# Taking a norm-and-gate epilogue out of a recurrent loop and running it over all token tiles at once, behind the loop

## The reference, cut to what matters

```python
def _step(S, xs):                      # once per token, per head
    qt, kt, vt, gt, bt = xs
    S = S * jnp.exp(gt)[..., None, None]
    delta = (vt - jnp.einsum('bhk,bhkv->bhv', kt, S)) * bt[..., None]
    S = S + jnp.einsum('bhk,bhv->bhkv', kt, delta)
    return (S, jnp.einsum('bhk,bhkv->bhv', qt, S))
...
o = gated_delta_rule(q, k, v, g, beta)                    # tokens, 6 heads, 64
o = o * rsqrt(mean(o * o, over the 64) + 1e-5) * norm_weight
o = o * silu(x @ Wg)
return o.reshape(tokens, 384) @ Wo
```

## Time and profile before

| what | value |
|---|---|
| median of three runs | 1545.75 us (1544.89 to 1547.8) |
| the profiled execution's own time | 1545.75 us |
| its span in the trace | 1544.0 us, 31244 instructions |
| outside the span | 1.75 us |
| PE busy / DVE busy / ACT busy / POOL busy | 87% / 60% / 44% / 20% of the span |
| the state block | about 554 to 599.8 us |

### The profile page before, as it was taken

How to read it: one execution, slowest core, us unless ns; L and a number is a source line. 1 busy time by engine, 2 the same in 40 slices (tenths; PEclk the granted TensorE clock), 3 DMA queues, 4 the chain that set the end, 5 groups by cost and what they waited for, 6 DMA issues and landing times. The chain is left out here.

```text
span 1544.0 us, 31244 instructions
## 1 busy us (share of the span) xinstructions
PE 1339.6 (87%) x12873; PEld 752.5 (49%) x12881; DVE 919.0 (60%) x2164; ACT 681.9 (44%) x987; POOL 305.8 (20%) x394
## 2 busy tenths in 40 slices
PE   7999997987150998899999989999789999989999
PEld 3355544553130877363555545436235555555436
DVE  3899965744886246665999935433445555535431
ACT  5578786634250223644777762111334444442110
POOL 4340440001308000006100000110333434210110
PEclk9999998998665599998999998999679999998999
DMA  3222200000312100003222030000300000000000
GB/s 89 59 42 62 61 2 32 1 12 0 103 41 51 28 5 1 14 1 64 38 37 40 13 100 0 1 9 0 62 10 16 14 16 14 9 1 1 0 0 28
DMA packets 51808, 41.64 MB, mean 27 GB/s; under 512 B 26498, under 2 KB 41971, under 8 KB 51667
## 3 DMA queue, kind: packets, MB, share of 16 engines
q1 hardware_dynamic: 51666, 39.65, 11.9%
HBM read 20.33 MB, written 3.43 MB: 15 GB/s over the span
## 5 line engine op out<-in xcount | busy, mean ns | idle before, releaser
L586 DVE TENSOR_REDUCE row_max_pieces<-psum 128x1 f32<-128x512 f32 (+3 forms) x672 | 407.2, 647 | 125.0 <-PE psum L481 122.6
L685 ACT ACTIVATE probs<-psum 128x1024 f32<-128x1024 f32 (+7 forms) x384 | 343.8, 900 | 219.8 <-PE psum L481 219.4
L535 PE MATMUL psum<-probs,v_ones 128*32 128x256 f32 (+1 forms) x2688 | 239.3, 377 | 8.6 <-POOL probs L470 4.2
L481 PE MATMUL psum<-q_all,k_head 97*32 97x512 f32 (+3 forms) x1536 | 193.8, 497 | 3.5 <-issue 3.5
L481 PE MATMUL psum<-k_stack,q_stack 96*32 96x512 bf16 x2048 | 162.6, 387 | 5.5 <-DVE row_max_pieces L586 3.3
L481 PE MATMUL psum<-q_stack,k_stack 97*32 97x512 bf16 x2048 | 160.8, 385 | 0.0
L535 PEld LDWEIGHTS psum<-probs,v_ones 128*32 128x32 f32 x2688 | 88.6, 109 | 85.1 <-POOL probs L470 21.2
L481 PE MATMUL psum<-k_head_bf,q_all_bf 80*32 80x512 bf16 (+3 forms) x768 | 96.6, 349 | 5.2 <-POOL q_all_bf L2314 3.7
L481 PEld LDWEIGHTS psum<-q_all,k_head 97*32 97x32 f32 x1536 | 79.2, 110 | 34.9 <-issue 9.3
L481 PEld LDWEIGHTS psum<-k_stack,q_stack 96*32 96x32 bf16 x2048 | 58.2, 97 | 71.9 <-DVE row_max_pieces L586 20.4
L481 PEld LDWEIGHTS psum<-q_stack,k_stack 97*32 97x32 bf16 x2048 | 59.5, 97 | 50.7 <-issue 3.8
(11 more groups left out here) (324 smaller groups left out, 2096.0 us busy)
## 6 DMA issues: line engine op xcount, KB each, us to landing
q_stack<-arena SPq DMA_DIRECT2D x32, 96.0 KB, 2.7
k_stack<-arena SPq DMA_DIRECT2D x32, 96.0 KB, 2.7
arena<-gd_g_sums SPq DMA_DIRECT2D x6, 512.0 KB, 5.9
q_stack<-arena SPq DMA_DIRECT2D x32, 64.0 KB, 2.3
k_stack<-arena SPq DMA_DIRECT2D x32, 64.0 KB, 2.3
x_tokens<-in_x SPq DMA_DIRECT2D x4, 256.0 KB, 4.2
k_stack<-arena SPq DMA_DIRECT2D x32, 32.0 KB, 2.3
q_stack<-arena SPq DMA_DIRECT2D x32, 32.0 KB, 2.0
```

What stands on the lines that cost most here:

```text
L481: last = pe.matmul(o[j:j + 32], by[:, j:j + 32], rows, **flags)
L535: last = pe.matmul(psum[32 * g:32 * g + VW, PVB, a - g * D:D], V[:, c, h, :], pr[:, n % PB, a:(g + 1) * D], start=(c == 0), stop=(c == (2 ...
L586: last = dve.reduce_max(mx[:, h % 2, qt, i:i + 1], o[:, 0:plain], AX.X)
L685: act.activation(pr[:, n % PB, q_from(c):], psum[:, 2 * (n % 2):2 * (n % 2) + 2, :].rearrange("p a n -> p (a n)")[:, q_from(c):], ACT.Exp, ...
```

## The change

Four things are done.

1. POOL's eight multiplications of `SG` by the norm weight leave the gate block. The weight's load now counts on the semaphore of `Wo`'s load.
2. The state loop loses its norm: ACT's Square and Sqrt, DVE's `mean_squares` and `norm_and_gate`. ACT keeps only the copy of the outputs.
3. The wait of DVE for the constant `own_block` moves from tile 0's state spread to ahead of the loop.
4. A new block stands between the state block and `project_out`. In it POOL multiplies `SG` by the weight, eight instructions of 128x384, and DVE does the whole norm over 128x3072 in a chain in which nearly each instruction waits for the one before.

```diff
@@ gate block, gpsimd
-                            pool.wait_ge(nw_loaded, 16)
-                            for t in range(NT):
-                                pool.wait_ge(gate_out, t + 1)
-                                gated = SG[:, t].rearrange("p (h c) -> p h c", c=GV)
-                                pool.tensor_tensor(gated, gated, nw[:].unsqueeze(1).broadcast_to([P, GH, GV]), ALU.mult)
@@ state block, vector
+                        dve.wait_ge(own_in, 16)
                         dve.wait_ge(blocked, 2)
                         for t in range(NT):
...
-                            if t >= 1:
-                                mean_squares(t - 1)
...
-                            if t == 0:
-                                dve.wait_ge(own_in, 16)
...
-                            if t >= 1:
-                                norm_and_gate(t - 1)
-                        mean_squares(NT - 1)
-                        norm_and_gate(NT - 1)
@@ state block, scalar
                         for t in range(NT):
                             act.wait_ge(o_in, t + 1)
-                            if t >= 2:
-                                act.wait_ge(summed, t - 1)
-                            act.activation(sq[:, t % 2], psum[:, 2 + t % 2, 0:VWD], ACT.Square).then_inc(squared, 1)
                             act.activation(O[:, t, :], psum[:, 2 + t % 2, 0:VWD], ACT.Copy).then_inc(o_kept, 1)
-                            act.wait_ge(ms_done, t + 1)
-                            act.activation(ms[:, t], ms[:, t], ACT.Sqrt).then_inc(rooted, 1)
@@ new block
+                with nc.Block() as block:
+                    @block.gpsimd
+                    def _(pool):
+                        for t in range(NT):
+                            pool.tensor_tensor(SG[:, t].rearrange("p (h c) -> p h c", c=GV),
+                                               SG[:, t].rearrange("p (h c) -> p h c", c=GV),
+                                               nw[:].unsqueeze(1).broadcast_to([P, GH, GV]), ALU.mult).then_inc(sw, 1)
+                    @block.scalar
+                    def _(act):
+                        act.wait_ge(to_act, 1)
+                        act.activation(ms[:], ms[:], ACT.Sqrt).then_inc(from_act, 1)
+                    @block.vector
+                    def _(dve):
+                        n = [0]
+                        def link(i):
+                            n[0] += 1
+                            i.then_inc(ch, 1)
+                            dve.wait_ge(ch, n[0])
+                        link(dve.tensor_tensor(sq[:], O[:], O[:], ALU.mult))
+                        link(dve.reduce_sum(ms[:], sq[:].rearrange("p t (h c) -> p (t h) c", c=GV), AX.X))
+                        dve.tensor_scalar(ms[:], ms[:], 1.0 / GV, RMS_EPS, ALU.mult, ALU.add).then_inc(to_act, 1)
+                        dve.wait_ge(from_act, 1)
+                        link(dve.reciprocal(rr[:], ms[:]))
+                        link(dve.tensor_tensor(O[:].rearrange("p t (h c) -> p (t h) c", c=GV),
+                                               O[:].rearrange("p t (h c) -> p (t h) c", c=GV),
+                                               rr[:].unsqueeze(2).broadcast_to([P, NT * GH, GV]), ALU.mult))
+                        dve.wait_ge(sw, NT)
+                        dve.tensor_tensor(O[:], O[:], SG[:], ALU.mult)
```

More of the change, by code:

```diff
@@ L1062, in gated_delta @@
         QET = sb("qe_features", [P, 2, S])
-        wload, nw_loaded = sem("wo_loaded"), sem("norm_weight_loaded")
+        wload = sem("wo_loaded")
         with ExitStack() as mid_scope:
@@ L1142, in loads @@
                         sp.dma_start(nw[:], d["nw"].rearrange("(a n) -> a n", a=1).broadcast_to([P, GV])
-                                     ).then_inc(nw_loaded, 16)
+                                     ).then_inc(wload, 16)
                         sp.dma_start(dtb[:], d["dt"].rearrange("(a n) -> a n", a=1).broadcast_to([P, GH])
@@ L1152, in _ @@
                             loads(sp)
-                            sp.wait_ge(wload, 16)
-                            sp.wait_ge(nw_loaded, 16)
+                            sp.wait_ge(wload, 32)
                             sp.wait_ge(head_loads, 32)
@@ L1628, in gated_delta @@
                 U = sb2("u", [P, 2, VWD])
[L1629 to L1634, removed]
                 s0, u_in, u_kept, s_in, s_done, o_in, o_kept = (sem(n) for n in
@@ L1681, in _ @@
                     def _(dve):
[L1682 to L1697, removed]
                         dve.memset(St[:], 0.0).then_inc(s0, 1)
@@ L1734, in _ @@
                             act.wait_ge(o_in, t + 1)
-                            if t >= 2:
-                                act.wait_ge(summed, t - 1)
-                            act.activation(sq[:, t % 2], psum[:, 2 + t % 2, 0:VWD], ACT.Square).then_inc(squared, 1)
                             act.activation(O[:, t, :], psum[:, 2 + t % 2, 0:VWD], ACT.Copy).then_inc(o_kept, 1)
-                            act.wait_ge(ms_done, t + 1)
-                            act.activation(ms[:, t], ms[:, t], ACT.Sqrt).then_inc(rooted, 1)
+            with ExitStack() as tmp2:
+                sb2 = lambda n, shape, dt=F32: core.sb(n, shape, dt, tmp2)
+                sq = EA.rearrange("p c n -> p (c n)")[:, 0:NT * VWD].rearrange("p (t n) -> p t n", t=NT)
+                ms, rr = sb2("o_mean_squares", [P, NT * GH]), sb2("o_inverse_rms", [P, NT * GH])
+                ch, sw, to_act, from_act = sem("norm_chain"), sem("gate_weighted"), sem("rms_in"), sem("rms_out")
+                with nc.Block() as block:
[26 more added lines that the diff above has]
+                        dve.tensor_tensor(O[:], O[:], SG[:], ALU.mult)
```

## The result

The changed kernel took 1563.95 us as the median of four runs (1560.65 to 1567.48); the kernel before, beside it, 1546.32 us (1544.89 to 1547.8). The ratio is 1.0115, with a 95% interval of 1.0087 to 1.0144: slower, as forecast. Besides these four the result lists 18 more executions of the changed kernel, the profiled one (1568.8) among them; all 22 have a mean of 1564.4, from 1556.35 to 1571.83. The median lies 1.45 us above the top of the forecast range and 3.65 above the forecast itself.

The account below looks back on a forecast made before the run. PE was taken to bound the state loop, with only tile 7's norm showing. New block 17.5 - 2.15 (earlier start) - 0.80 (gate block) = +14.55 us on 1545.75 gave 1560.3 us, range 1556.8 to 1562.5.

Parts of the forecast that it names:

- The loop is PE's; the norm in it is free: State loop: PE, busy 39.47 of 40.20 us, bounds it; only tile 7's norm is on the path, 2.93 us.
- The rival that taking the norm out speeds up the loop: State loop: the norm's work was holding PE up, so removing it brings the kernel within 0.2%; chance 2%.
- Part 1: Gate block's end: without POOL's multiplications it ends with DVE, 0.80 us earlier.
- Part 2: State loop without norm: period stays 5.26 us; DVE starts the new block 2.15 us before the old end.
- Part 3: Ahead of the state loop: the wait for `own_block` costs nothing, ending 0.66 us before DVE is first needed.
- Part 4: New block: DVE's chain takes 14.5 us alone, 17.5 us with POOL's multiplications beside it.
- the mutual hold: New block: POOL and DVE's two-input multiplies hold each other up, block takes 17.5 us; chance 51%, 1560.3 us.
- rivals without a hold: New block: POOL and DVE do not hold each other up, +11.55 us, 1557.3 us; chance 13%.
- one-sided one: New block: DVE is held by POOL, POOL not by DVE's multiplies, +12.6 us, 1558.3 us; chance 22%.
- PE and its clock: Projection's restart after the longer pause: 0, with 1 us either way, and as much again for later layers.
- The sum against its base: Whole kernel: +14.55 us added to the profiled execution's 1545.75 us gives 1560.3 us.
- The range: Whole kernel: 1556.8 to 1562.5 us, leaving out about 1 in 10.

Follow-up runs that it names:

- experiment 3: Changed kernel with POOL's eight weight multiplications left in the gate block, none in the new block: 1557.01 us, ratio 1.0062 to the kernel before.
- experiment 4: Changed kernel plus 114 PE transposes into an unused bank during the new block, to keep PE awake: 1563.6 us, ratio 1.0096 to the kernel before.
- experiment 2: Kernel before plus only a block of six DVE memsets between state block and projection, as a pause: 1566.46 us, ratio 1.0113.
- experiment 1: Changed kernel run and traced again, no edit: 1562.55 us, ratio 1.0092 to the kernel before.
- experiment 5: Kernel before against itself, no edit: 1549.16 us against 1549.02, ratio 1.0001.
- experiment 7: Kernel before, no edit, third and fourth look: 1548.70 and 1549.88 us.

## Why the prediction was wrong, step by step

*The loop is PE's; the norm in it is free.* Right. The copies of `U` take the same 36.70 us from first to last, with DVE idle 2.23 ahead of the last one instead of 0.95. The rival that taking the norm out speeds up the loop is wrong: it gave nothing.

*Part 1, -0.80.* Measured 0.81.

*Part 2, DVE starts 2.15 us ahead of the old end.* Right where the clock is the same: in the second trace the last copy of `U` is at 592.12 and DVE starts at 596.37, 4.25 later; before it was 6.38 to the end of the norm. That is 2.13. In three of the five traces of the changed kernel, PE's clock fell already during tile 7; the windows view of the first shows PEclk at half:

```profile
594.00:597.00 3.00, 2.67 (x9) 1.73 (x8) 0.30 (x2) 0.29 (x1) 0.00 (x0) 0.50 0.00 0
```

and that cost 1.2 to 1.35 us each time. In experiments 3 and 4, which have the same loop, it did not happen, nor in any of the four traces of before or in experiment 2. Three of seven against none of five: whether that is chance is open.

*Part 3, the earlier wait.* Nothing: DVE's first copy has the same 1.30 us idle, released by PE.

*Part 4, the chain of 14.5 us, 17.5 with the mutual hold.* 14.52 without POOL (experiment 3), 17.36 with. The case that no row of before showed, POOL held by a DVE multiply with two SBUF inputs, is shown: 4.11 and 4.13 us for instructions of 0.98. The rule of the Trainium skill (SBUF — State Buffer, "SBUF: two separate sides") gave just this, and here the trace agrees. The rivals without a hold or with a one-sided one (1557.3, 1558.3) were wrong in mechanism.

*PE and its clock, 0 within 1 us.* From the first copy of `U` to the first addition the sum says 17.5 - 2.15 = 15.35; the mean over five traces is 16.1, 0.8 more, nearly all of it from the clock's early fall in tile 7. So this term was put too low by 0.8, and not for the restart that it was meant for. The restart itself was hardly dearer: 6.76 us on average (5.88 to 7.11) from first transpose to first addition, 6.63 before. Nor is it always at half clock: in experiment 1's trace PEclk from 614.00 to 620.00 is 0.70.

*The sum against its base.* This is the step that failed: "1545.75 + 14.55". The profiled execution and the three runs shown lay between 1544.9 and 1547.8, and I took them for the kernel's time and their spread for its spread. Over all 71 runs of the kernel before on record the mean is 1548.5 us with a standard deviation of 2.9; over all 41 of the changed kernel (the 23 of the result and of the experiments without an edit, and the 18 others named with the result) it is 1563.8 with 4.1. The base was thus 2.75 us too low. The difference is 15.3, with a standard error of 0.7; the 23 alone give 14.8 with 0.9. The forecast's difference was 14.55, and the parts as measured give 16.1 - 0.8 = 15.3. So the miss of 3.65 us is 2.75 from the base and, by the traces, 0.8 from the clock's early fall in tile 7; the runs alone can't tell 15.3 from 14.55. That leaves nothing beyond some 1 us for the later layers. On the base of 1548.5 the forecast's own sum gives 1563.1 us.

*The range.* It allowed 1 us for the restart and 1 us for the later layers, and nothing for the base. The layers ahead of and behind the change differ by 4 us and 8 us between executions. As an estimate: three runs of a kernel with a standard deviation of 2.9 leave its mean uncertain by 1.7 us, and a median of four with 4.1 is off by some 2; together that is 2.6, and two of these above 1560.3 put the top at about 1565.5. The first trace, 23 us longer, sets a lucky execution of before beside an unlucky one after (1568.8 against a mean of 1563.8). The first ratio, 17.6 us, overstates the change through before alone: its four runs have a mean of 1546.3, 2.2 under the kernel's, while the four of the changed kernel, at 1564.0, are ordinary.

What stays open: why the 255 matmuls of one layer run at 0.62 in one execution and 0.66 in the next. The traces show only that PE's busy time changes and that of DVE, ACT and POOL does not, and nothing here sets it.

## What to carry to other kernels

Work of another engine that lies under the bound engine is free in the loop and dear behind it, even if large shapes make it cheaper: some 22 us of DVE and ACT work (eight tiles of 2.0 and 0.7 us), of which only tile 7's showed, became 17.4 us behind the loop that all show, and the kernel got slower by 15. When POOL and DVE both work on SBUF, as in this block, add up the times of POOL's instructions and of DVE's two-input ones instead of laying them side by side: that gave 17.5 us where 17.36 were measured, and side by side gave 14.5. And ask of a baseline how far two executions of it differ, place by place, before giving a range to 0.2%: a gap that a second trace of the same program also shows is not the change's.

## What the runs showed of the hardware that was not expected

- One program's executions differ by 11 us in 1548 (1542.72 to 1554.12 over 71 runs), and PE's busy time goes with them: 430.51 against 421.24 us for the same 4755 matmuls, at a mean clock of 0.84 against 0.85 (experiments 5 and 7).
- A DVE memset of 128x3072 that waited on the semaphore of the one before it started 0.71 us after that one's recorded end, where the sum chained to the square of the same width started 0.03 us after it (experiments 2 and 3). From start to start the memsets stand 3.32 us apart (601.94 to 605.26), the square and the sum 3.39, so the gap may be the memset's own work outside its recorded time; no run separates the two.
- The small scale instruction on 128x48 took 0.33 us beside POOL and 0.19 without (605.12 in the first trace, 604.71 in experiment 3): with only one SBUF input it seems to wait for POOL as well. The sum over 128x3072 took 3.35 either way, and POOL beside it 0.98.
- Twelve transposes put into a gap of PE kept its clock at 1.00 through the restart, and the tail came out 1.3 us shorter than was expected from the work moved (45.74 against 47.0 at best).
